# Flamingo decoder kernel: the shared expert's down projection moved ahead of the routed experts' tile loop

## The reference, cut to what matters

```python
xg = flat[tok_table]                                   # tokens gathered by expert and slot
g = jnp.einsum('ecd,efd->ecf', xg, gate_w)
u = jnp.einsum('ecd,efd->ecf', xg, up_w)
y = jnp.einsum('ecf,edf->ecd', jax.nn.silu(g) * u, down_w)
out = jnp.zeros_like(flat).at[tok_table.reshape(-1)].add((y * w_table[..., None]).reshape(-1, d))
sg = jnp.einsum('nd,sfd->nsf', flat, sh_gate_w)
su = jnp.einsum('nd,sfd->nsf', flat, sh_up_w)
out = out + jnp.einsum('nsf,sdf->nd', jax.nn.silu(sg) * su, sh_down_w)   # the last product is what moves
```

## Time and profile before

| | |
|---|---|
| median of 3 runs | 658.81 us (657.25 to 660.98) |
| profiled execution, span | 652.8 us |
| profiled execution, time of its own | not given; the span lies 6.0 us under the median and 4.5 us under the fastest run |
| PE busy | 501.9 us (77% of the span) |
| DVE busy | 389.4 us (60%) |
| ACT busy | 275.4 us (42%) |
| POOL busy | 144.4 us (22%) |
| the routed experts' loop on PE | 136.8 to 196.5 us of the span |

### The profile page before, as it was taken

One profiled execution on the slowest core, in us unless ns is written; L12 is line 12 of the kernel. 1 busy time (PEld: TensorE's weight loads), 2 busy tenths in 40 slices (PEclk: granted clock), 3 DMA queues, 4 the chain that ended last, 5 costly groups with the idle time before them and its releaser, 6 DMA issues.

```text
span 652.8 us, 7578 instructions
## 1 busy us (share of the span) xinstructions
PE 501.9 (77%) x2570; PEld 347.6 (53%) x2578; DVE 389.4 (60%) x1083; ACT 275.4 (42%) x512; POOL 144.4 (22%) x138
## 2 busy tenths in 40 slices
PE   2999886869997237876777879999997766755674
PEld 1788752358883113434344445788884444633442
DVE  6544368911111556766567558522459899999844
ACT  1100144112321134478597741233456762334765
POOL 4000037790005763000303123000023011011200
PEclk9999977969999565887899976999999997965867
DMA  8880011026977170299994000000000000000000
GB/s 283 268 307 2 0 39 57 18 59 221 334 180 136 44 101 5 52 261 219 106 120 124 2 1 1 2 0 1 1 0 1 1 1 1 1 1 0 17 21 28
DMA packets 52886, 49.14 MB, mean 75 GB/s; under 512 B 7070, under 2 KB 45092, under 8 KB 52848
## 3 DMA queue, kind: packets, MB, share of 16 engines
q1 hardware_dynamic: 49776, 44.92, 29.0%
q0 software_dynamic: 3072, 3.75, 2.2%
HBM read 40.71 MB, written 12.58 MB: 82 GB/s over the span
## 4 chain that ended last, share of the span: by engine, by line
PE 38%; DVE 28%; issue 8%; DMA 7%; ACT 6%; SPq 6%; POOL 6%; POOLq 0%; DVEq 0%; ACTq 0%
PE bank L1338 5%; PE bank L1420 4%; PE bank L1348 4%; DVE big L1045 3%; SPq L390 3%; PE bank L1599 3%; POOL xg_rows L510 3%; PE bank L1442 2%; DVE top L1048 2%; DMA SH<-query_parts 2%; DVE bnst L576 2%; PE bank L1613 2%; PE bank L1638 2%; PE bank L1622 2%; DMA query_parts<-ar 2%
## 5 line engine op out<-in xcount | busy, mean ns | idle before, releaser
L470 POOL TENSOR_TENSOR rstd<-ve,neghalf 128x2 f32<-128x2 f32 x32 | 25.7, 804 | 260.8 <-DVE ve L581 260.6
L863 DVE SCALAR_TENSOR_TENSOR HM<-bank,HM 128x384 f32<-128x384 f32 x64 | 35.6, 556 | 50.0 <-ACT HM L1187 41.4
L1185 ACT ACTIVATE HM<-bank,ATN 128x256 f32<-128x256 f32 x64 | 31.3, 490 | 40.3 <-PE bank L1522 39.6
L537 POOL DMA_INDIRECT WK<-y_rows,slot x32 | 33.3, 1039 | 66.5 <-DMA y_rows<-ph 53.9
L1533 PE MATMUL bank<-HM 128*32 128x256 f32 x128 | 43.4, 423 | 4.1 <-ACT HV L1169 2.3
L1320 PE MATMUL bank<-identf,HN 128*128 128x128 f32 x96 | 18.2, 327 | 33.7 <-DVE HN L586 33.6
L1515 PE MATMUL bank<-CMP,sel 96*128 96x256 bf16 x64 | 19.2, 300 | 31.2 <-DVE HM L863 14.1
L546 POOL TENSOR_TENSOR rs<-vr,neghalf 128x32 f32<-128x32 f32 x4 | 22.1, 5522 | 94.8 <-DVE vr L847 94.8
L1072 ACT ACTIVATE HT<-bank 128x512 f32<-128x512 f32 x24 | 14.0, 598 | 67.4 <-PE bank L1320 67.4
L741 DVE TENSOR_TENSOR he<-sil,bank 64x64 f32<-64x64 f32 x32 | 7.0, 219 | 54.4 <-ACT sil L1119 54.2
L510 POOL DMA_INDIRECT xg_rows<-HN,slot x32 | 32.8, 1026 | 21.6 <-DVE slot L707 12.5
(11 more groups left out here) (293 smaller groups left out, 1262.3 us busy)
## 6 DMA issues: line engine op xcount, KB each, us to landing
big<-in_eg SPq DMA_DIRECT2D x8, 512.0 KB, 7.5
big<-in_eu SPq DMA_DIRECT2D x8, 512.0 KB, 7.5
big<-in_ed SPq DMA_DIRECT2D x8, 512.0 KB, 8.1
xg_rows<-zer SPq DMA_DIRECT2D x1, 2048.0 KB, 8.6
ph<-xg_rows SPq DMA_DIRECT2D x16, 128.0 KB, 3.5
y_rows<-ph SPq DMA_DIRECT2D x16, 128.0 KB, 4.3
WK<-key_parts SPq DMA_DIRECT2D x16, 128.0 KB, 8.0
big<-key_parts SPq DMA_DIRECT2D x16, 128.0 KB, 6.6
```

Of the source, the lines that this page charges most:

```text
L470: pool.tensor_tensor(rstd[:, b, :], ve[:, b, :], neghalf[:, 0:TB], ALU.pow)\
L537: pool.indirect_dma_start(out=G4[:, q, k, :], out_offset=None, in_=y_dram, in_offset=bass.IndirectOffsetOnAxis(slot[:, t, k:k + 1], 0), bo ...
L863: dve.scalar_tensor_tensor(out=dcs[:, 2 + i % 3, :], in0=bank[4 + i % 2][:, 0:384], scalar=DH ** -0.5, in1=dcs[:, i % 2, :], op0=ALU.mult, ...
L1185: act.activation(dcs[:, i % 2, 0:S], bank[2 + i % 2][:, 0:S], ACT.Exp, bias=ATN[:, 0, 32 * b + h:32 * b + h + 1])
```

## The change

PE does all sixteen `shared_out` pieces in one block, behind the wait for HS and ahead of the loop's first transposes. DVE does its four additions of the result ahead of its first `he` in place of one each at turns 4, 8 and 12 and one behind the loop. Nothing is added or removed. PE's, DVE's and the banks' semaphores keep their counts. The streams of ACT, POOL and SP are not touched.

```diff
@@ the DVE stream
+            for b in range(B):
+                add_shared(b)
 
             for t in range(ST):
                 q = t % 2
@@
                 last.then_inc(s["s_he"], 1)
-                if t % (2 * TB) == 0 and t > 0:
-                    add_shared(t // (2 * TB) - 1)
-
-            add_shared(B - 1)
@@ the PE stream
             pe.wait_ge(s["s_hs"], 2 * NF)
+            for t in range(ST):
+                shared_out(t)
             for t in range(ST + 2):
                 if t < ST:
                     experts_turn(t)
-                    shared_out(t)
                 if 1 <= t <= ST:
                     experts_in(t - 1)
                 if t >= 2:
                     experts_out(t - 2)
```

## The result

The changed kernel is slower: 662.22 us (median of 20 runs, 657.35 to 665.24) against 657.36 for the kernel before (20 runs, 652.26 to 662.15), a ratio of 1.0081 with a 95% interval of 1.0056 to 1.0106. That is 5.3 us. The forecast was 654.3, 4.5 us faster. The profiled execution of the changed kernel took 661.47 us and its span is 659.7, against 652.8 before; the two profiles lie 6.9 us apart, the medians 4.9.

A forecast was written before the change was run, and what follows sets the result against it. PE's wait for rows, then its products, were taken to bound the loop, with the DMA queue binding its end after the change. Loop end 196.5 to 192.0 gains 4.5 us: 658.8 - 4.5 = 654.3 us, 8-in-10 range 650.5 to 657.4.

The forecast's parts named there:

- The bound, the idle time and the block's place: Ahead of the loop: PE idles 9.0 us for rows; the block, needing only HS, starts at 130.46 and covers 6.3 us.
- the low end of what I gave: Loop turns without shared products: 2.68 us at the low end, 2.79 us taken, against 3.55 us now.
- I take it that the clock holds: Gap ahead of the block: PE keeps full clock through the remaining 2.7 us, saving 2.7 us of half-speed ramp.
- my two reasons: For the clock holding ahead of the block: a 2.13 us gap kept it; the present gap's first 2.69 us stand at 1.00.
- What is late next: the DMA queue: Late loop: 29.4 us from first reload (153.6) to tile 14's landing at 183.0, so PE waits 2.5 us.
- The rival of the rigid queue: Late loop: first reload to tile 14's landing stays 32.4 us, loop ends at 195.0, gain 1.5 us, 657.3; chance 0.12.
- The rates that this step was summed from: DMA queue in the loop: 10.3 MB need 30.5 us at 338 GB/s or 28.8 us at 357 GB/s.
- I take nothing for them: DVE's four additions beside the block cost nothing; uncovered, waits would cost up to 0.7 us each at two places.
- The wait that PE got in return: Late loop: PE waits 2.5 us for tile 14's rows, then needs 9.0 us to the loop's end at 192.0.
- the slower case: Gap ahead of the block: clock falls and stays down, the block takes 27.8 us, time 668.2 us; chance 0.05.
- Nothing behind the loop has a fixed time near it: Behind the loop: context products, second stack of keys and gather start from its end, so all 4.5 us pass on.

The follow-up runs named there:

- e1: Changed kernel with the three key stores moved from turn 8 to 12 and the first stack of keys behind the loop: 659.04 us, ratio 1.0036 to before.
- e3: Changed kernel with two unused products added in each of turns 8 to 15 (7 us in all): 657.50 us, ratio 1.0035 to before.
- e5: Changed kernel with unused products filling PE's waits ahead of tiles 13 and 14 (6.1 us of work): 656.15 us, ratio 0.9986 to before.
- e12: Changed kernel (full block) with key stores in turn 12 and both stacks of keys behind the gather: 653.25 us, ratio 0.9941 to before.
- e2: Kernel before with the key stores moved to turn 12 and the first stack of keys behind the loop: 661.47 us, ratio 1.0100.
- e6: Changed kernel with three unused products in PE's wait for HS ahead of the block: 662.27 us, ratio 1.0106 to before.
- e4: Changed kernel with half the block: batches 0 and 1 ahead of the loop, 2 and 3 in turns 8 to 15: 649.44 us, ratio 0.9927 to before.
- e10: Changed kernel with three quarters of the block: batches 0 to 2 ahead, 3 in turns 12 to 15: 657.28 us, fast-run ratio 0.9960 to before.
- e11: Changed kernel with a quarter of the block: batch 0 ahead, 1 to 3 in turns 4 to 15: 650.82 us, ratio 0.9911 to before.
- e9: Kernel before with the second stack of keys issued after the first stack of queries: 655.73 us, ratio 0.9992.
- e7: Changed kernel with the second stack of keys issued after the first stack of queries: 658.47 us, ratio 1.0010 to before.
- e8: Half block ahead of the loop, with the second stack of keys issued after the first stack of queries: 647.22 us, ratio 0.9865 to before.

## Why the prediction was wrong

**The bound, the idle time and the block's place: right.** PE was idle for the rows, HS was the block's only need, the block starts at 130.44 (forecast 130.46), and the turns took 2.68 us, the low end of what I gave.

**"I take it that the clock holds": wrong in this profile, and open in general.** Four profiles have such a gap ahead of the block: behind those of 2.74 (changed), 2.75 (e1) and 2.74 us (e3) the clock fell, behind the one of 2.76 (e5) it held. One of my two reasons could not carry the step: that the first 2.69 us of the present gap stand at 1.00 says nothing of what comes next. The changed kernel's gap stands at 1.00 too, and the fall comes a microsecond into the block. It cost the first reload 1.3 us against the forecast (154.9, not 153.6).

**"What is late next: the DMA queue": right place, wrong size.** I took 29.4 us from the first reload to tile 14's landing, since I believed that the queue had slack between the first chunks. It was 32.3. The rival of the rigid queue had that, at 0.12. That step cost 2.9 us. Over the kernels with the keys in the loop the interval lies between 29.8 and 34.1 us; in those with short turns and no keys (e1, e12) it is 25, and with long turns and no keys (e2) 29.0. So the key traffic made the rows late. e1 takes away both the stores, which stand ahead of the last chunk in SP's order, and the first stack, which stands behind the rows, and doesn't part the two. The DMA share of 0.95 in the earlier trace rows should have been read as nearly full: in the changed kernel 10.7 MB (331 GB/s for 32.3 us) went at a share of 1.04.

The rates that this step was summed from were misread as well. The stretch of the earlier trace rows is not the one with the most bytes. Two microseconds later the kernel before moved 393 GB/s:

```profile
172.00:182.00 10.00, 10.00 (x77) 8.64 (x76) 1.61 (x5) 2.73 (x9) 0.00 (x0) 1.00 1.06 393
```

At that rate the 10.3 MB need 26.2 us, less than the 26.9 that PE left, and by it my own sum would have had no wait. So it is in part luck that the wait came where I forecast it. No single rate gives the time: the changed kernel moved 382 GB/s from 170 to 180, the 383 that I said would be asked of it, and only 132 from 184 to 187.24, at a share of 1.21, while loads of the first stack and tile 14's rows were under way.

**"I take nothing for them", DVE's additions: right in the changed kernel**, where no record of the block waits for one; in e6 one such wait was 0.16 us and in e12 1.00, both with DVE late.

**The wait that PE got in return: priced as idle time alone. This is the step that failed.** I had PE wait 2.5 us and then run at full clock to the end in 9.0 us. It waited 1.68 and 2.28 us and then took 15.5, since the clock fell in the first wait and stayed down for the rest of the loop: 6.5 us more than forecast. I had weighed a fallen clock only in the gap ahead of the block, and had put the slower case there. I never asked the same question of the wait that my own sum created. e5 shows the step by itself: with the waits filled the same stretch took 8.7 us.

The Trainium skill, page "TensorE: Matmul & The Clock Gate", section "HAM oscillation", warns of this, bursts of products that wait for a DMA and start at the lower rate; this case's trace agrees as far as the fall goes, with 3.5 us for sixteen records in place of 1.9.

**"Nothing behind the loop has a fixed time near it": true, but it was not enough.** The second stack of keys is issued at the loop's end and shares the engines with the gather. In the profile before the gather took 8.1 us and looked like POOL's own pace; in the changed kernel it took 11.5. Since the last store's landing was 0.9 us quicker, 2.5 us of this counts.

The sum, against the span's first gathered addition: forecast 4.5 sooner; plus 1.3 (the block's clock), 2.9 (the queue; together the 187.3 in place of 183.0), 6.5 (the loop's clock), 2.5 (the gather) gives 8.7 later; measured 8.9. All of it is still there at the last store of layer 1's queries (325.0 and 334.0); some 2 us are gone by the end of the span, and I have not found where. And the profile before is a quick one (its span is 2.8 us under what the median of 20 runs would leave, taking the 1.8 us between time and span from the changed kernel's profile), which is why the medians differ by less than the profiles.

That the gather is longer in the changed kernel by its own doing isn't shown. It took 9.9 to 11.2 us in e3, e4, e5, e6, e10 and e11 too, and e9 says that the kernel before had little to lose there. Why it took 8.1 in the profile before, with the stack issued 4.0 us ahead of the gather, and 11.0 in e4, with 3.7, stays open.

## What to carry to other kernels

When work is moved out of a loop that runs beside a stream of loads, the loop asks for the same bytes in less time; count the time from the first reload to the last row that is needed, and don't expect it to shrink with the turns if the engines are already nearly full (here a share of 0.95, and 29.8 to 34.1 us with turns long or short), and move only what that leaves room for. Here a quarter of the work gave 0.9%, half of it 0.7%, and all of it cost 0.8%. A wait that a change creates on TensorE has to be priced with the clock that it may lose: 6.5 us here, beside 4.0 of idle time; work that keeps it busy can be cheaper than none. And a queue is a place too: taking the keys out of it brought the rows 7 us sooner, and put behind the loop they made the gather 5 us longer in e1 and 9 in e2.

## What the runs showed of the hardware

- Once fallen in the loop, the clock stayed at 1.2 GHz until the loop's end, from about 180 to 203 us, though from tile 14's transposes on PE had no wait at all (busy 15.54 of 15.54 us at 0.50, 187.29 to 202.83); e6 and e7 show the same. In the block, behind the first gap, it was back in less than 4 us (131.8 to 135.2), and in the kernel before within 5.33; there PE was at products of 256 columns, in the late turns of the changed loop mostly at ones of 64. Why it stayed down wasn't tried.
- Whether a wait made the clock fall did not follow from its length: it fell at ones of 1.26 (e6), 1.68 (changed), 1.76 (e7), 2.74 (changed, e3) and 2.75 us (e1) and held at ones of 1.94 (e10), 2.13 (before) and 2.76 (e5). It can also fall when the wait is over and PE is at work again, as in the changed kernel's block.
- DVE's additions of 16 columns took 0.16 to 0.17 us in the changed kernel, and one of them 2.38 us in e12, from 133.19 to 135.57, just after POOL's cast ended (133.62 + 1.91 = 135.53); the copy behind it took 4.99 us in place of 1.23 and ended a microsecond after POOL's subtraction. The Trainium skill, page "SBUF — State Buffer", section "SBUF: two separate sides", says that POOL and DVE (DVE in a two-port mode or with two inputs in SBUF) hold a shared port pair by turns, for whole instructions, and that the one that starts first gets it. This trace agrees in that DVE's instructions ended only when POOL's were through. It doesn't show who started first: by the records the slow addition began 0.43 us ahead of the cast. It takes a late DVE: in the changed kernel's profile the copy ended at 131.9, and the cast began at 133.3. In e4, e7, e10 and e11, where DVE came 1.6 to 2.5 us later than that, one addition took 2.46 to 2.53 us and the copy its 1.23; in e6, e8 and e12, 2.4 to 3.1 us later, the copy took 4.99 too.
- Gathers issued by POOL, of rows of 1 KB, took 6.9 us to the first addition by themselves (e7, e8, e9, e12), 8.1 in the kernel before and 9.9 to 11.5 in the others beside a stack of 1 MB in runs of 512 bytes, and 17 beside two (e1, e2).
